# One VectorE instruction order, changed: six row searches and two weight writes are placed elsewhere in the period of an image

## The reference, cut to what matters

```python
scores, idx = jax.lax.top_k(sim, PK_TOPK)                  # 16 best on each of two sides
index = idx[0][..., :, None] + (idx[1] * 64)[..., None, :]
score = scores[0][..., :, None] + scores[1][..., None, :]
final_scores, pk_idx = jax.lax.top_k(score, 16)
final_indices = jnp.take_along_axis(index, pk_idx, axis=-1)   # the table rows
final_scores = softmax(final_scores)
k = jnp.einsum('bnhk,bnhkd->bnhd', final_scores, keys_table[final_indices + head * 4096])
v = jnp.einsum('bnhk,bnhkd->bnhd', final_scores, values_table[final_indices + head * 4096])
```

## Time and profile before

| | |
|---|---|
| time, median of 3 runs | 11988.08 us (11980.57 to 11988.49) |
| the profiled execution's own time | 11981.82 us |
| its span, first to last instruction | 11980.0 us |
| mean granted TensorE clock | 0.981 of full |
| PE busy | 11034.8 us (92%) |
| DVE busy | 10219.1 us (85%) |
| POOL busy | 8419.7 us (70%) |
| ACT busy | 7851.7 us (66%) |

### The profile page before, as it was taken

The page is one execution under the profiler, slowest core; times in us unless marked ns, Lnnn a source line. Parts: engine busy times, 40 slices in busy tenths (PEclk is TensorE's granted clock), DMA queues, the critical chain, the costliest instruction groups (busy, mean ns, idle before and its releaser), DMA issues.

```text
span 11980.0 us, 263894 instructions
## 1 busy us (share of the span) xinstructions
PE 11034.8 (92%) x70396; PEld 9154.4 (76%) x70396; DVE 10219.1 (85%) x42192; ACT 7851.7 (66%) x17926; POOL 8419.7 (70%) x8196
## 2 busy tenths in 40 slices
PE   3999999999999999999999999999999999999999
PEld 2777777777777777777777777777777777777777
DVE  6889888888888898888888988888889888888883
ACT  2666666666666666666666666666666666666665
POOL 0677777677777777777777777767777777777776
PEclk6999999999999999999999999999999999999999
DMA  2566566565565665665655656656556566566554
GB/s 66 155 173 179 156 174 171 160 175 167 166 177 159 171 179 157 171 172 161 175 166 164 177 158 170 179 155 174 170 161 177 165 168 177 158 172 177 158 170 137
DMA packets 1651836, 1975.58 MB, mean 165 GB/s; under 512 B 336238, under 2 KB 1125870, under 8 KB 1649902
## 3 DMA queue, kind: packets, MB, share of 16 engines
q1 hardware_dynamic: 1387950, 1418.48, 40.8%
q0 software_dynamic: 262144, 537.40, 17.2%
HBM read 1881.20 MB, written 73.40 MB: 163 GB/s over the span
## 4 chain that ended last, share of the span: by engine, by line
PE 57%; DVE 19%; ACT 8%; issue 7%; DMA 6%; SPq 2%; POOL 0%; DVEq 0%; ACTq 0%; POOLq 0%
PE bank L1008 16%; PE bank L1044 10%; PE bank L1031 6%; PE bank L1018 5%; DVE decay L1579 4%; PE bank L891 4%; ACT bank L1255 4%; DMA moving<-keyspace 3%; DVE apart L1709 3%; DMA wide<-states 3%; DVE onehot L1804 2%; PE bank L995 2%; PE bank L972 2%; DVE decay L1588 2%; PE bank L1060 2%
## 5 line engine op out<-in xcount | busy, mean ns | idle before, releaser
L819 POOL DMA_INDIRECT gath<-in_table_dram,rowsT x8192 | 8419.5, 1028 | 3533.0 <-issue 2449.9
L1262 ACT ACTIVATE weight<-bank 128x512 f32<-128x512 f32 x4096 | 2441.0, 596 | 2895.2 <-PE bank L1018 2863.6
L1008 PE MATMUL bank<-weight,rowtab 128*128 128x256 f32 x16384 | 4263.0, 382 | 0.0
L1008 PEld LDWEIGHTS bank<-weight,rowtab 128*128 128x128 f32 x16384 | 3122.9, 191 | 756.2 <-issue 20.6
L1255 ACT ACTIVATE bank<-bank,seventeen 128x512 f32<-128x512 f32 x4096 | 2711.5, 662 | 14.7 <-PE bank L1018 11.5
L1044 PEld LDWEIGHTS bank<-spread,gath 128*128 128x128 f32 x16384 | 2160.3, 192 | 149.6 <-issue 14.5
L1044 PE MATMUL bank<-spread,gath 128*128 128x96 f32 x16384 | 2116.5, 272 | 5.5 <-DMA gath<-in_table_dram,rowsT 5.1
L1031 PE MATMUL bank<-moving,pick_b 96*128 96x512 bf16 x4096 | 1584.5, 387 | 485.1 <-ACT bank L1255 392.4
L1018 PE MATMUL bank<-moving,pick_b 96*128 96x512 bf16 x4096 | 1562.2, 381 | 81.3 <-DMA moving<-keyspace 80.7
L1579 DVE TENSOR_TENSOR_SCAN decay<-decay,wide 128x256 f32<-128x256 f32 x2048 | 1238.4, 670 | 3.3
L1031 PEld LDWEIGHTS bank<-moving,pick_b 96*128 96x128 bf16 x4096 | 438.1, 107 | 924.6 <-ACT bank L1255 738.3
(11 more groups left out here) (268 smaller groups left out, 16949.8 us busy)
## 6 DMA issues: line engine op xcount, KB each, us to landing
rowtab<-in_tableD_dram SPq DMA_DIRECT2D x2048, 256.0 KB
wide<-states SPq DMA_DIRECT2D x512, 512.0 KB
moving<-keyspace SPq DMA_DIRECT2D x4096, 64.0 KB
gath<-in_table_dram,rowsT POOLq DMA_INDIRECT x8192
moving<-keyspace SPq DMA_DIRECT2D x4096, 32.0 KB
pix<-in_x_dram SPq DMA_DIRECT2D x504, 256.0 KB
keyspace<-split SPq DMA_DIRECT2D x256, 256.0 KB
out_dram<-acc SPq DMA_DIRECT2D x64, 64.0 KB
```

Source lines behind the costliest of these rows:

```text
L819: pool.indirect_dma_start(out=gath[:, u % RING, j, :], out_offset=None, in_=table, in_offset=bass.IndirectOffsetOnAxis(ap=rowsT[k][:, col: ...
L1008: mm(dense_ps[:, 0:TOK], rowtab[:, r, s % 2 * 2 + half, :], weight[s % 2][:, half * TOK:(half + 1) * TOK], start=(s % 16 == 0 and half == ...
L1262: ins = af(weight[s % 2][:], zd_ps[s % 2][:], ACT.Exp, scale=-1.0)
```

## The change

Only the string DVE_ORDER differs. No instruction is added or removed; DVE runs the same items in another sequence.

```diff
-1 F.ps+2 F.g+1
+1 F.ps+2 S.R3+0 F.g+1
 2 S.e6+0 S.e7+0
 3 F.h2+1 S.re3+0
 4 
-5 a6.3-1 S.n0+1 S.n1+1 S.lo3+0 S.R7+0
-6 F.rf+2 a6.5-1
-7 a6.6-1 S.T0+1
-8 
-9 
+5 a6.3-1 S.n0+1 S.n1+1 S.lo3+0
+6 F.rf+2 a6.5-1 S.R4+0
+7 S.R5+0 S.R6+0
+8 S.R7+0 S.wb1+0
+9 a6.6-1 S.T0+1
...
-16 S.T11+1 S.T12+1
+16 S.T11+1 S.T12+1 S.wb3+0
...
-29 S.wb3+0 S.L0+1 F.h1+2 S.L1+1
+29 S.L0+1 F.h1+2 S.L1+1
...
-46 S.R2+1 a3.3+0
+46 a3.3+0
...
-59 S.R3+1 a5.3+0
+59 a5.3+0
 60 
 61 S.wb0+1 S.e5+1 a5.5+0
-62 S.R4+1 S.lo2+1 S.R5+1
-63 S.wb1+1 S.R6+1
+62 S.lo2+1
+63 S.R2+1
```

## The result

| | before | changed kernel |
|---|---|---|
| time, median of 4 runs each | 11984.33 us (11968.62 to 11988.49) | 12160.76 us (12144.86 to 12166.39) |
| ratio, 95% interval | | 1.0148 (1.0130 to 1.0165) |
| profiled execution, its span | 11981.82 us, 11980.0 us | 12162.40 us, 12160.6 us |
| mean granted TensorE clock | 0.981 | 0.976 |

The changed kernel is 1.5% slower. The forecast, 12085 us, had the direction and the place. The time lies 76 us above it and 11 us above the end of the range.

What follows compares the result with a forecast made beforehand. The prediction took PE, busy 92% of the span, as the bound, without slack at L954 in most borders. From 11981.8 us, +120 - 30 - 40 + 55 = +105 gave 12087, stated as 12085 us, range 11985 to 12150.

Steps and rivals of the forecast that it cites:

- The strand and its missing slack: Rows 1 to 3: L954 has no slack behind L1602 in 42 of 57 borders, so R3 makes PE wait there.
- 2.46 us less the gap that was there: R3 between F.ps and F.g delays L954 by its length less the existing gap at each border: +120 us.
- The waits at L948, -30: Period border: with searches gone from the period's end DVE is early, and 30 of 32.2 us of waits go.
- what is not waited for now cannot be won: Period border, L948: the gain is bounded by the waits there, 32.2 us in all.
- R4 to R7 and wb1 in the hole, 0: Between a6.5 and a6.6: 9.3 us of work hidden in DVE's wait for PE, costing nothing, margin about 0.6 us.
- The relief, -40: R2 out of row 46, wb3 out of row 29: DVE earlier, PE gains 0.65 us a period, -40 us.
- The clock, +55: Behind the new stand at L954 TensorE's clock falls; 0.6 of the 91 us upper bound taken, +55 us.
- Rival 1: The clock falls at every border, or a6.6 is overrun: 12143 us, chance 0.14.
- Rivals 2 and 3: Second half: relief worth 80 us without clock drop, 11992 us, chance 0.12; or 148 us, 11924 us, chance 0.12.
- Rival 4: Slower by less: no drop of the clock, rest as forecast, 12032 us; within the forecast's range, no chance of its own.

Runs made afterwards that it cites:

- e1: Changed kernel with R3 two places earlier, between F.y and a5.6 instead of F.ps and F.g: 11924.72 us, 0.9953 of the kernel before.
- e2: Changed kernel with R4 also between F.ps and F.g, right behind R3: 12318.19 us, 1.0291 of the kernel before.
- h7: e1 with R3 moved into the hole of rows 6 to 9, ahead of R4: 12000.18 us, 1.0022 of the kernel before.
- i1: The order of e1 run again in a later comparison: 11925.33 us, 0.9961 of the kernel before.
- i8: e1 with R2 back in row 46 and wb3 back in row 29: 11898.38 us, 0.9943 of the kernel before.
- e4: Changed kernel with R2 back in row 46 and wb3 back in row 29: 12150.8 us, 1.0155 of the kernel before.
- h5: e1 with the three weight writes wb1, wb2, wb3 between F.ps and F.g: 11974.48 us, 1.0001 of the kernel before.
- e3: Kernel before with R2 moved from row 46 to row 59, ahead of R3, and wb3 from row 29 to 16: 12184.37 us, ratio 1.0180.
- e8: The order of i8 on a chip where every kernel took about a quarter longer: 15138.37 us, 0.9999 of the kernel before there.

## Why the prediction was wrong in its size

- **The strand and its missing slack: right.** The prediction said that PE had no slack at L954 although it did not wait there, and that R3 would turn into a wait of about 2.4 us, some 150 us over the run. It is 145.0 us in 62. e1 shows that this place is the cause of the loss, e2 that the loss grows with the work put there.
- **"2.46 us less the gap that was there", +120: too low by 23 us.** L954 stands 143 us more. I took off the 1.0 to 2.4 us between L1602 and L954 in 15 of the 57 borders and in the five early ones as slack. The stand is at its full 2.2 to 2.5 us in those too. At the earlier trace rows one sees what the gap was: PE waited 0.83 us at L948, then ran L1008 at half rate, and came to L954 late for that. In each of the 15 a half-rate stretch begins between L948 and L954, and in none of the other 42. The change takes the wait away, with it the half-rate stretch, and with that the gap. Two terms were not independent.
- **The waits at L948, -30: right** (-31). But "what is not waited for now cannot be won" was not: with the waits also went the half-rate stretches behind them, 19 of 61 borders with 75 us at half rate, worth some 37 us by half of that time.
- **R4 to R7 and wb1 in the hole, 0: right.** DVE waits 0.60 and 0.70 us for PE at `a6.6` in the two kinds of border. I had worked out a margin of 0.6 us. h7 shows what lies beyond: 1.6 us a period.
- **The relief, -40: this step failed most.** The wait at row 50 went, as foreseen (129 waits at L1060 to 69, -22 us), and then PE waits longer for key loads (+13 us). That the scan loads could leave at most 1 us sooner was right: it is 0.7 us (i1 against i8). Against e4 the sum is nothing, and between i1 and i8 it is 27 us the wrong way, with intervals that overlap. My own argument had said that the key loads stand behind the scan loads; I still took 0.65 us a period from waits that DVE causes, as if PE would not wait for the next thing in the queue.
- **The clock, +55: right in sign, too low by 20 us.** PE's busy time grew by 75 us for the same matmuls. Read stretch by stretch in the record of the granted clock, from 400 us on, half rate grew from 232 us in 55 stretches to 393 us in 88; half of the difference is 80 us. I had weighed the new stand at 0.6 of the borders. The clock falls behind it in 49 of 61, and the net is less than 91 because the 19 old stretches behind L948 are gone. The Trainium skill (page TensorE: Matmul & The Clock Gate, section HAM oscillation — how this bites in real kernels) describes a kernel in which PE waits for a transfer in each iteration and each next one starts at the lower rate. The changed kernel's trace comes near to that, with 49 of 61; h5 and h7, with 0.8 and 1.5 us in every period and no lower clock behind them, show that a recurring wait alone does not do it.
- **The sum.** Waits of PE: +143 - 31 - 22 + 13, and +10, -10, +5 at L1031 for ACT, L1031 for issue and L938: +108 us. With 75 us of clock this is 183 us; the spans differ by 180.6. Forecast: +105. Of the missing 76 the relief (-40 forecast, -22 + 13 measured) is about 31, the gap 23, the clock 20.
- **The rivals.** Rival 1 came nearest (12143 us: every border pays for the clock), though `a6.6` was not overrun. Rivals 2 and 3 gave the relief 80 and 148 us and are out by e4 and i8. Rival 4, no drop of the clock, is out by the mean clock. Its number is near in part by luck: it kept the +120 and a relief of -20, and had the clock at +91. My range went to 12150 and left out that a clock falling at most borders could meet a relief of nothing.

## What to carry to other kernels

- A list of waits does not show slack of nothing. Before you put work into an engine's order, compare the end of each producer behind it with the start of its consumer on the bottleneck engine. At 0.05 us the bottleneck pays for every microsecond, here 1.4 to 1.6 times over with the clock. Two places earlier the same 2.46 us were free.
- Look for the hole on the strand itself: work belongs ahead of an instruction that waits for PE (`a5.6`, 4.8 us), not behind it.
- A gap that comes out of a stall is not slack if the change removes the stall, and a relief in front of a queue is worth what the next thing in the queue allows; here 0.7 us sooner bought only longer waits one load on. Take both from the row behind the wait, not from the wait.

## What the runs showed that I had not expected

- **The same stand costs differently by its length and place.** At L954 2.3 to 2.4 us cost 1.6 per microsecond, 0.8 us cost about its length. At L1060 in row 9 1.5 us cost its length or less, with no lower clock behind any of 61. At L948 waits of 1.5 us (the median of e3, whose clock falls in 42 of 61 borders), and some of 0.5 to 0.8 us in before, do have a half-rate stretch behind them. So the length of a wait alone does not decide. Whether the narrow matmuls around L948 and L954 do was not tested.
- **1.98 us of DVE at the end of the period cost 3.4 us a period** (e3), 1.7 us for each microsecond of search.
- **On two chips the kernel took 25% longer**, and there ACT stood still for long times without a releaser on this core (`remote`), and PE behind ACT or without a releaser at all (`issue`). Waits of e8 (15138.37 us):

```profile
ACT weight L1262 <- remote: 1954.5, 561, 7.2
PE bank L1031 <- ACT bank L1255: 1021.5, 679, 6.7
PE bank L1031 <- issue: 437.5, 320, 4.3
```

The three entries are 0, 400.3 and 75.6 us in i8, the same order of work on another chip. The cause is open. An edit that orders DVE's work is judged differently there, so a ratio from one chip need not hold on another.
